# Recurrence stage of a four-layer kernel: deviation per token on four columns, and all low halves of the context keys formed by GpSimd

## Time and profile before

| | us |
|---|---|
| median of three runs | 5328.55 |
| their lowest and highest | 5319.98, 5329.23 |
| profiled execution | 5320.13 |
| its span | 5318.5 |
| busy in the span: PE, DVE, ACT, POOL | 4723.6, 3735.3, 2931.1, 2013.1 |

### The profile page before, as it was taken

The page is one execution under the profiler, slowest core; times in us unless marked ns, Lnnn a source line. Parts: engine busy times, 40 slices in busy tenths (PEclk is TensorE's granted clock), DMA queues, the critical chain, the costliest instruction groups (busy, mean ns, idle before and its releaser), DMA issues. The chain is left out here.

```text
span 5318.5 us, 75415 instructions
## 1 busy us (share of the span) xinstructions
PE 4723.6 (89%) x28818; PEld 1691.3 (32%) x28818; DVE 3735.3 (70%) x4684; ACT 2931.1 (55%) x5418; POOL 2013.1 (38%) x912
## 2 busy tenths in 40 slices
PE   5886998998688799997899999997789999996899
PEld 2332444443233233332322222221333333331344
DVE  6768999998453677772499999994567777771421
ACT  3553444444232366664288888886326666665432
POOL 0116666665000388885000000000008888886000
PEclk9897999999799799999999999998899999998999
DMA  2334434343220433322211111111424232212100
GB/s 99 125 138 132 116 103 114 112 113 89 92 65 33 89 69 69 69 57 97 87 29 32 32 32 33 33 33 47 134 87 99 58 77 61 65 45 76 64 24 16
DMA packets 474865, 391.90 MB, mean 74 GB/s; under 512 B 175151, under 2 KB 372628, under 8 KB 474472
## 3 DMA queue, kind: packets, MB, share of 16 engines
q1 hardware_dynamic: 474496, 387.00, 26.6%
HBM read 246.50 MB, written 139.34 MB: 73 GB/s over the span
## 5 line engine op out<-in xcount | busy, mean ns | idle before, releaser
L2803 DVE TENSOR_REDUCE att_part<-att_scores 128x2 f32<-128x802 f32 x1024 | 953.4, 986 | 108.6 <-PE att_scores L2642 96.8
L2776 ACT ACTIVATE att_prob<-att_lower 128x512 f32<-128x512 f32 (+1 forms) x1664 | 883.5, 596 | 128.4 <-PE att_lower L2656 107.4
L3610 DVE TENSOR_REDUCE att_part<-att_scores 128x1 f32<-128x423 f32 x1280 | 675.8, 590 | 219.3 <-PE att_scores L3313 219.2
L3554 ACT ACTIVATE att_prob<-att_lower 128x512 f32<-128x512 f32 (+1 forms) x1088 | 563.3, 602 | 243.9 <-PE att_lower L3325 242.0
L3594 POOL TENSOR_TENSOR att_acc<-att_acc,att_prob 128x1024 f32<-128x1024 f32 (+2 forms) x240 | 671.1, 2796 | 51.8 <-ACT att_prob L3554 22.6
L2379 DVE TENSOR_REDUCE att_part<-att_scores 128x1 f32<-128x401 f32 x1024 | 515.4, 567 | 161.9 <-PE att_scores L2193 161.7
L1373 POOL TENSOR_TENSOR scan_z<-scan_r,scan_states 128x512 f32<-128x512 f32 x256 | 469.6, 1839 | 337.4 <-DVE scan_states L1450 323.2
L2671 PE MATMUL att_lower<-att_prob,att_v 128*32 128x256 f32 (+1 forms) x6144 | 523.6, 413 | 19.7 <-issue 19.7
L2318 ACT ACTIVATE att_prob<-att_scores 128x512 f32<-128x512 f32 (+1 forms) x832 | 430.8, 601 | 195.3 <-PE att_scores L2205 195.2
L2790 POOL TENSOR_TENSOR att_out<-att_sums_sb,att_spread 128x512 f32<-128x512 f32 x32 | 40.7, 1272 | 1164.1 <-DMA att_spread<-recips 1164.1
L2359 POOL TENSOR_TENSOR att_acc<-att_acc,att_prob 128x1024 f32<-128x1024 f32 (+2 forms) x176 | 450.2, 2558 | 68.8 <-ACT att_prob L2318 56.4
(11 more groups left out here) (431 smaller groups left out, 7896.4 us busy)
## 6 DMA issues: line engine op xcount, KB each, us to landing
v<-scan_val SPq DMA_DIRECT2D x96, 256.0 KB, 2.3
att_v<-v SPq DMA_DIRECT2D x32, 768.0 KB
att_spread<-recips SPq DMA_DIRECT2D x64, 256.0 KB
mix_plane<-in_mask SPq DMA_DIRECT2D x16, 800.5 KB, 6.5
att_k<-k1hi SPq DMA_DIRECT2D x32, 400.2 KB
att_k<-k3hi SPq DMA_DIRECT2D x32, 400.2 KB
scan_x<-in_ctx_t SPq DMA_DIRECT2D x12, 1024.0 KB, 5.7
o<-att_out SPq DMA_DIRECT2D x32, 256.0 KB, 2.0
```

The source lines that it names most:

```text
L2776: nc.scalar.activation(prob[g % NP][0:kw(kt), h, :], scores2[0:kw(kt), n % RING2, :], ACT.Exp).then_inc(exped, 1)
L2803: nc.vector.reduce_max(part[q % 2][:, :, ec, piece], scores1[:, bank["unit", p], :, 0:PIECE], AX.X).then_inc(reduced, 1)
L3554: nc.scalar.activation(prob[g % NP][0:kw(kt), h, :], scores2[0:kw(kt), n % RING2, :], ACT.Exp).then_inc(exped, 1)
L3610: nc.vector.reduce_max(part[q % 2][:, hc, piece:piece + 1], scores1[:, bank["piece", p], 0:PIECE], AX.X).then_inc(reduced, 1)
```

## The change

- The deviation is formed per token once instead of on all 128 rows. In "std", TensorE now multiplies the sums of squares, as the stationary operand, by one column of the matrix of 1/512: the tokens come to lie on the partitions, 128 at a time, so 512 tokens fill four columns. ScalarE takes the square root of these four columns, VectorE their reciprocal (`invert`).
- A new group "spread" brings them back: four products whose stationary operand is such a column, repeated 128 times, with the identity. ScalarE drains it into `std`, and `normalise` multiplies by it. "spread" stands one k3 group after "std" and costs as much as "std" in `group_cost`, by which `when` changes for some groups by one step.
- The low halves of the keys go from VectorE to GpSimd, one chunk (128 x 512) at a time: one for k2, four for k3, four for k1 per tile, each two steps after its group, behind that step's state product. k1's last two chunks come after the next tile's sums of squares. `halves` now counts nine per tile, and the waits for it are set to that.

```diff
@@ group_order / group_cost
             if o == std_behind(t):
                 yield t, "std", 0
+            if o == std_behind(t) + 1:
+                yield t, "spread", 0
             yield t, "k3", o
-    if what in ("mean", "std"):
+    if what in ("mean", "std", "spread"):
         return 1.0 * t.n / KT
...
@@ SyncE
-                    sp.wait_ge(halves, 3 * t.t + nth)
+                    sp.wait_ge(halves, LOWS * t.t + 1 + C * (nth - 1))
...
@@ TensorE
+                def square_means(t):
...
+                    for j, wd in enumerate(t.width):
+                        ins = nc.tensor.matmul(psum[0:wd, made % CR, j:j + 1], total[1][:, j * P:j * P + wd], k["mean"][:, 0:1],
+                                               start=True, stop=True)
...
+                def spread_rows(t):
...
+                    for j, wd in enumerate(t.width):
+                        ins = nc.tensor.matmul(psum[:, made % CR, j * P:j * P + wd], rowinv[0:wd, j:j + 1].broadcast_to([wd, P]),
+                                               k["ident"][0:wd, 0:wd], start=True, stop=True)
...
                         elif what == "std":
                             pe.wait_ge(totalled, 2 * t.t + 2)
-                            group([(k["mean"][:], total[what == "std"][:, 0:t.n])], n=t.n)
+                            square_means(t)
+                        elif what == "spread":
+                            pe.wait_ge(inverted, t.t + 1)
+                            spread_rows(t)
@@ ScalarE
-                        act.wait_ge(normed, t.t)
-                    drain(std[:, 0:t.n], ACT.Sqrt, n=t.n, bias=k["eps5"][:])
+                        act.wait_ge(inverted, t.t)
+                    m = t.width[0]
+                    drain(rowstd[0:m, 0:len(t.width)], ACT.Sqrt, m=m, n=len(t.width), bias=k["eps5"][0:m])
+
+                def drain_spread(t):
+                    if t.t:
+                        act.wait_ge(normed, t.t)
+                    drain(std[:, 0:t.n], ACT.Identity, n=t.n)
...
@@ GpSimd
+                def key_low(t, name, o, full, hi_, lo_):
+                    n = t.n
+                    pool.wait_ge(drained, end(t.t, name, o))
+                    if o == 0 and t.t:
+                        pool.wait_ge(kstored[name], 32 * t.t)
+                    nc.gpsimd.tensor_tensor(lo_[:, o, 0:n], full[:, o, 0:n], hi_[:, o, 0:n], ALU.subtract).then_inc(halves, 1)
...
+                    for t in tiles:
+                        after = tiles[t.t + 1] if t.t < LAST else None
+                        yield when[t.t, "k2", 0] + 2
+                        key_low(t, "k2", 0, k2f, k2hi, k2lo)
...
+                        for o in range(C):
+                            yield when[t.t, "k3", o] + 2
+                            key_low(t, "k3", o, kf, hi[0], lo[0])
+                        for o in range(2):
+                            yield when[t.t, "k1", o] + 2
+                            key_low(t, "k1", o, kf, hi[1], lo[1])
...
+                        for o in range(2, C):
+                            yield when[t.t, "k1", o] + 2
+                            key_low(t, "k1", o, kf, hi[1], lo[1])
@@ VectorE
+                def invert(t):
+                    m = t.width[0]
+                    dve.wait_ge(drained, end(t.t, "std", 0))
...
+                    nc.vector.reciprocal(rowinv[0:m, 0:len(t.width)], rowstd[0:m, 0:len(t.width)]).then_inc(inverted, 1)
+
                 def normalise(t):
                     n = t.n
-                    dve.wait_ge(drained, end(t.t, "std", 0))
-                    nc.vector.reciprocal(std[:, 0:n], std[:, 0:n]).then_inc(inverted, 1)
-                    dve.wait_ge(inverted, t.t + 1)
+                    dve.wait_ge(drained, end(t.t, "spread", 0))
                     nc.vector.tensor_tensor(xc[:, :, 0:n], xc[:, :, 0:n], bc(std[:, 0:n], C), ALU.mult).then_inc(normed, 1)
...
                     for t in tiles:
-                        yield when[t.t, "k2", 0] + 2
-                        key_low(t, "k2", k2f, k2hi, k2lo)
-                        yield when[t.t, "std", 0] + 2
+                        yield when[t.t, "std", 0] + 1
+                        invert(t)
+                        yield when[t.t, "spread", 0] + 2
                         normalise(t)
-                        yield when[t.t, "k3", C - 1] + 2
-                        key_low(t, "k3", kf, hi[0], lo[0])
...
-                        yield when[t.t, "k1", C - 1] + 2
-                        key_low(t, "k1", kf, hi[1], lo[1])
```

More of the change, by code:

```diff
@@ L956, in scan_and_keys @@
         tiles = [Stretch(t) for t in range(B * TILES)]
-        LAST = len(tiles) - 1
+        LAST, LOWS = len(tiles) - 1, 1 + 2 * C
         ends, when, cost, count = {}, {}, {}, 0
@@ L996, in scan_and_keys @@
         mean, std = ph.sb("mean", [P, KT]), ph.sb("std", [P, KT])
+        rowstd, rowinv = ph.sb("rowstd", [P, KT // P]), ph.sb("rowinv", [P, KT // P])
         pairsum, total = ph.sb("pairsum", [P, 2, KT]), [ph.sb(f"total{i}", [P, KT]) for i in range(2)]
@@ L1173, in group @@
                     made += 1
+                def square_means(t):
+                    nonlocal made
+                    if made >= CR:
+                        pe.wait_ge(drained, made - CR + 1)
+                    for j, wd in enumerate(t.width):
+                        ins = nc.tensor.matmul(psum[0:wd, made % CR, j:j + 1], total[1][:, j * P:j * P + wd], k["mean"][:, 0:1],
+                                               start=True, stop=True)
+                    ins.then_inc(product, 1)
+                    made += 1
+                def spread_rows(t):
+                    nonlocal made
+                    if made >= CR:
+                        pe.wait_ge(drained, made - CR + 1)
+                    for j, wd in enumerate(t.width):
+                        ins = nc.tensor.matmul(psum[:, made % CR, j * P:j * P + wd], rowinv[0:wd, j:j + 1].broadcast_to([wd, P]),
+                                               k["ident"][0:wd, 0:wd], start=True, stop=True)
+                    ins.then_inc(product, 1)
+                    made += 1
                 def key_group(t, weight, half, o):
@@ L1308, in keys @@
                         if t.t:
-                            act.wait_ge(halves, 3 * t.t - 2)
+                            act.wait_ge(halves, LOWS * (t.t - 1) + 1)
                             act.wait_ge(kstored["k2"], 32 * t.t)
@@ L1317, in keys @@
                         if t.t:
-                            act.wait_ge(halves, 3 * t.t)
+                            act.wait_ge(halves, LOWS * t.t)
                             act.wait_ge(kstored["k3"], 32 * t.t)
@@ L1325, in keys @@
                                 drain_std(t)
+                            if o == std_behind(t) + 1:
+                                yield when[t.t, "spread", 0] + 1
+                                drain_spread(t)
                             yield when[t.t, "k3", o] + 1
@@ L1339, in keys @@
                                 affine_full(t)
-                        act.wait_ge(halves, 3 * t.t + 2)
+                        act.wait_ge(halves, LOWS * t.t + 1 + C)
                         if t.t:
@@ L1396, in keys @@
                     add_halves(tiles[0], 1)
[L1397 to L1408, removed]
+                    for t in tiles:
+                        after = tiles[t.t + 1] if t.t < LAST else None
+                        yield when[t.t, "k2", 0] + 2
+                        key_low(t, "k2", 0, k2f, k2hi, k2lo)
+                        if after:
+                            yield when[t.t, "k3", 0]
+                            pool.wait_ge(arrived[after.t % 2], 16 * (after.t // 2 + 1))
+                            add_pairs(after, 0)
+                            yield when[t.t, "k3", 0] + 1
+                            add_halves(after, 0)
+                        for o in range(C):
[4 more added lines that the diff above has]
+                            key_low(t, "k1", o, kf, hi[1], lo[1])
+                        if after:
+                            yield when[t.t, "k1", 2] + 3
+                            pool.wait_ge(squared, after.t + 1)
+                            add_pairs(after, 1)
+                            yield when[t.t, "k1", 2] + 4
+                            add_halves(after, 1)
+                        for o in range(2, C):
+                            yield when[t.t, "k1", o] + 2
+                            key_low(t, "k1", o, kf, hi[1], lo[1])
                 more = keys()
@@ L1487, in x_low @@
                     nc.vector.tensor_tensor(xs.lo[:, :, 0:n], x[t.t % 2][:, :, 0:n], xs.hi[:, :, 0:n], ALU.subtract).then_inc(xsplit, 1)
+                def invert(t):
+                    m = t.width[0]
+                    dve.wait_ge(drained, end(t.t, "std", 0))
+                    if t.t:
+                        dve.wait_ge(drained, end(t.t - 1, "spread", 0))
```

(5 more changed lines are left out.)

## The result

The changed kernel takes 5384.1 us (median of 5375.8 to 5387.1), the kernel before 5328.4 beside it: ratio 1.0106, interval 1.0093 to 1.0119, that is +56 us where the sum gave +38. Predicted were 5362 us, in a range of 5322 to 5402. The direction and the stage are those of the forecast. In the profiles, the time from the first scan to the end of the last is 961 us instead of 903. What follows takes 4007 us instead of 3999, and in the profiles of all variants it lies between 3998 and 4007 without order.

The account below looks back on a forecast made before the run. The prediction took turns at a port shared by VectorE and GpSimd to bound the recurrence. Its terms, -66 + 133 - 12 - 15 - 8 + 6, gave +38 us and a forecast of 5362 us, range 5322 to 5402.

Parts of the forecast that it names:

- the sum: Whole change, in the recurrence stage: -66 + 133 - 12 - 15 - 8 + 6 = +38 us.
- The bound: Recurrence stage: instructions taking turns at a shared port fill about 830 of 903 us, 92%; TensorE stands close behind.
- turns: Recurrence: scans, wide two-operand VectorE passes and every GpSimd instruction run one at a time; the change adds net +67 us.
- the second rival: Far slower: GpSimd falls behind, late state products stop ScalarE, TensorE, then VectorE; +48 on top of +38, 5410 us; chance 0.11.
- The low halves: Keys' low halves: leaving VectorE takes off 66 us of turns, coming to GpSimd in chunks adds 133.
- The columns: Four-column deviation, reciprocal and "spread": reciprocal credit -12 us, new wait +6, TensorE's added passes 0 as covered.
- The new wait: TensorE stands at "spread" until VectorE inverts four columns: some 4 us in each batch's first tile, taken as +6 us.
- the reciprocal's credit: VectorE's wide reciprocals, 42 us, shrink to four columns; they take no turn, so only -12 us, bounds 0 and -42.
- TensorE's passes: Deviation product replaced by 16 passes: +2 us per full tile, 24 in all, counted as 0 because covered.
- The credits for waiting: Recurrence: chunks fill time GpSimd waits for scans, -15 us, and time VectorE waits for TensorE's spread values, -8 us.
- Faster: Rival: VectorE's own time is the wall and GpSimd's chunks run beside it; -47 us, 5279 us; chance 0.07.
- no change: Rival: chunks fit into time that no one holds, with all credits against the cheapest chunks; 5320 to 5337 us; chance 0.20.

Follow-up runs that it names:

- The fill: Changed kernel with the keys' low halves left out, each GpSimd chunk replaced by a zero fill of about its length that reads nothing; 1.0012 of the kernel before.
- the scan from PSUM: Kernel before, with the outer product written back into its PSUM bank and read there by the scan: 0.9954; the changed kernel with the same edit: 0.9987.
- the four kernels with and without them: Changed kernel (1.0106) and kernel before, and each with the keys' low halves left out, stored as zero: 0.9958 and 0.9928 of the kernel before.
- chunks alone: Kernel before with only the low halves moved to GpSimd in chunks, deviation and reciprocal as before; 1.0096, 5376.6 us.
- the columns alone: Changed kernel with the low halves back on VectorE, so only the four-column deviation and "spread" differ from the kernel before; 1.0034, 5343.3 us.
- the kernel without the wait: Kernel with the four-column deviation only, but "spread" multiplies constant columns and waits for nothing (normalisation left out); 0.9997 of the kernel before.
- more passes alone: Kernel before with eight more float32 passes of 128 columns ahead of each deviation product, results unused, no new wait; 1.0009, 5333.8 us.

## Why the prediction was right, point by point, and where it failed

**The bound** was right: turns at a shared port, not VectorE's busy time. The fill and the scan from PSUM show it; 114 us less of VectorE's busy time with a longer stage rules out VectorE as the wall. So VectorE and GpSimd meet not only at semaphores but also at this port. The bound was too simple all the same: 28 of the 78 us that the low halves cost on GpSimd are its queue, which the sum had left to the second rival. With the scans off the port the kernel gains only 25 us: TensorE, busy 805 of 889 us of the stage there, stands close behind, as I had written. The rule of the Trainium skill (SBUF — State Buffer, "Who interferes with whom") agrees in both directions: a GpSimd instruction that only writes is not held up (1174 ns at most), and a scan with one SBUF input doesn't contend (1282 at most).

**The low halves** came out in size by luck: +67 of turns less 23 of credits is +44; the four kernels with and without them give +40, though chunks alone cost 51. The two terms beneath were each too large: leaving VectorE brought 38 us, not 66, and coming to GpSimd cost 78, not 133 less 23 of credits. In both, a us of turns was worth some 0.6 us of time, and the errors cancel. The chunk was taken at 1.13 us and takes 1.15.

**The columns** are the step that failed. By the sum they brought -12 (reciprocal) + 6 (new wait) = -6 us; alone they cost 18, with the chunks 56 - 51 = 5. The new wait is the term that was wrong: I named TensorE at "spread" in a batch's first tile, at +6, and gave the other tiles nothing. In the columns alone most of the standing is in the tails (16.1 of 23.3 us), and without this wait the 18 us are gone. Whether the reciprocal's credit exists isn't shown: its instruction fell from 3.32 to 0.18 us, and the kernel without the wait is level with before although more passes alone cost +5, which leaves room for a credit of some 7 us and for none.

In the changed kernel another engine stops too, which I had not named: VectorE, whose queue is in order, at the four-column reciprocal, 27.1 us in 11 stops. How this comes about, at the start of a batch (GpSimd, ScalarE, VectorE; idle time and its releaser in brackets):

```profile
...
701.33 2.19 POOL L1421 TENSOR_TENSOR scan_total<-scan_pairsum 128x512 f32<-128x512 f32 x1
703.47 1.50 POOL L1428 TENSOR_TENSOR scan_lo<-scan_kf,scan_hi 128x65 f16<-128x65 f32 x2
...
706.16 2.07 POOL L1428 TENSOR_TENSOR scan_k2lo<-scan_k2f,scan_k2hi 128x512 f16<-128x512 f32 x1
708.19 2.34 POOL L1414 TENSOR_TENSOR scan_pairsum<-scan_x 128x1024 f32<-128x1024 f32 x1
710.49 1.26 POOL L1408 TENSOR_TENSOR scan_z<-scan_r,scan_states 128x512 f32<-128x512 f32 x1
...
715.16 2.08 POOL L1428 TENSOR_TENSOR scan_lo<-scan_kf,scan_hi 128x512 f16<-128x512 f32 x1
...
```

```profile
...
705.00 0.20 ACT L1264 ACTIVATE scan_states<-scan_initial 128x1 f32<-128x1 f32 x1 [7.84 <-POOL scan_lo L1428]
...
711.78 0.20 ACT L1264 ACTIVATE scan_states<-scan_initial 128x1 f32<-128x1 f32 x1 [4.17 <-POOL scan_z L1408]
711.89 0.25 ACT L1273 ACTIVATE scan_rowstd<-scan_psum,const_eps 128x4 f32<-128x4 f32 x1
...
```

```profile
...
712.17 0.18 DVE L1549 RECIPROCAL scan_rowinv<-scan_rowstd 128x4 f32<-128x4 f32 x1 [4.89 <-ACT scan_rowstd L1273]
...
714.84 1.44 DVE L1505 TENSOR_TENSOR_SCAN scan_states<-scan_w,scan_initial,scan_a 128x512 f32<-128x512 f32 x1
...
```

GpSimd forms the tail's last two chunks (703.47) behind the next tile's total. ScalarE must have them before it writes k3 over the tiles that they read; in its queue this wait stands ahead of a seed, and ScalarE is idle 7.84 us until 705.00. Then it waits 4.17 us more for the state product of 710.49, which is queued behind a chunk (706.16) and a pair sum. The chunks of 706.16 and 715.16 show the price beside a scan, 2.07 and 2.08 us. Only then does ScalarE drain the deviation (711.89), for which VectorE has been idle 4.89 us. Of the low halves' wait I had written that it has steps in hand, "about one after a tail tile", and put a lag there under the second rival; it took 19.2 us of ScalarE in three batch starts.

VectorE's idle time here is not the columns' price. The seed of 711.78 belongs to the scan of 714.84, which could not have begun before it whatever the reciprocal did. GpSimd's queue holds up both, and on top of the chunks the columns cost only some 5 us.

**TensorE's passes** were put at 24 us of busy time and at 0 in the sum, as covered. They did cost little (+5 by the kernel with more passes). TensorE's busy time rose by 30 us, but the passes are only some 17 of it: the new ones take 30.0 us, and what is left of the old line (mean and deviation together before, the mean alone now) fell from 31.1 to 18.1. The others are unchanged passes that last longer: with the chunks alone, where no pass was added, TensorE's busy time rises by 15 us too (822 for 807 from the first scan to the end of the last). Its granted clock in the stage is 0.93 of full speed instead of 0.95, and 0.85 instead of 0.94 in the tail. In that tail (columns as in the earlier trace rows) TensorE stands still from 665 to 670 us, and then runs at 0.50, the lower of its two levels:

```profile
...
665.00:670.00 5.00, 0.00 (x0) 0.00 (x0) 0.53 (x1) 0.63 (x4) 4.31 (x4) 0.92 0.38 61
670.00:675.00 5.00, 4.17 (x8) 1.69 (x9) 1.63 (x2) 0.69 (x2) 1.05 (x2) 0.50 0.54 193
...
```

The prediction has no term for this; how much of the 56 us the clock makes, no run separates.

**The credits for waiting** (-15 latency, -8 TensorE) were half wrong: GpSimd's waits for scans fell by 88 us, but VectorE's for TensorE rose by 100 and those for ScalarE by 37. A late state product makes drains, groups and spreads late, as at the batch start above; that all of it comes so is argued, not shown. This is the second rival's chain, in a mild form: ScalarE's waits for products went from 187.9 to 218.6 us, not to a multiple.

**The other rivals.** "Faster" falls with every run at the port; "no change" would have needed all the credits. Two slips in the working change nothing: 4 x 4 us is 16, not 17, and 47 us less than the forecast's base of 5324 is 5277, not 5279.

What stays open: how the 28 us that a fill still costs divide between the state products and ScalarE's drains, and why the chunks cost as little as 11 us in the same queue once the scans are off the port. A hint, not tested: in the kernel before with that scan ScalarE waits 43.4 us for state products instead of 187.9, so a product can come later before anyone waits for it.

## What to carry to other kernels

Before work goes from a busy engine to an idle one, look in the timeline at whether the two ever lengthen each other's instructions: if they take turns, the sum of turns bounds the stage, and a pass that takes longer on the other engine makes it longer. Then ask what the new instructions will stand in front of: in this kernel over a third of the price on GpSimd was its queue. Here an operand kept in PSUM took the scan off the port, and that was worth 25 us where moving work lost 56. A short reciprocal in place of a long one gained nothing here, because an engine had to stand in its queue for it.

## What I had not expected of the hardware

A fill on GpSimd of 1280 float32 columns takes 1.16 us, no more than a subtract of 512 columns. And the scan takes 1.25 to 1.28 us whether its operand comes from SBUF undisturbed or from PSUM: what the scans took beyond that before (their median was 1.70) was waiting.
